# An octonion FFN kernel: the statistics of the third group of rows in the opening, a dot product and a ternary step moved on VectorE

## The chip, the cores and the metric

The kernel runs on one core of a Trainium2 chip. What is measured is the device time of the whole program in microseconds. TensorE (PE) does the matmuls, VectorE (DVE), ScalarE (ACT) and GpSimd (POOL) the elementwise work, SyncE (SP) issues the DMAs. Each engine runs its own list of instructions in order, and the lists meet at semaphores.

## The reference, cut to what matters

```python
x = L0_attn_x                                  # 1 x 2048 x 1024, f32
xn = layernorm(x, eps=1e-5)                    # per row, over 1024
attn = autocorrelation(xn)                     # rfft, irfft of |f|^2, top 6 lags, softmax, rolled rows
def ternary_dequant(W):
    scale = mean(abs(W))
    return scale * clip(round(W / scale), -1, 1)
def oct_ternary_linear(xp, W):                 # 8 octonion components, signs of S_OCT
    M = einsum('jik,jod->koid', S_OCT, ternary_dequant(W))
    return einsum('...id,koid->...ko', xp, M)
gate = oct_ternary_linear(xn, w_gate)          # 8 x 342 x 128
up   = oct_ternary_linear(xn, w_up)            # 8 x 342 x 128
h    = silu(gate) * up
out  = oct_ternary_linear(h, w_down)           # 8 x 128 x 342
return x + attn + out
```

The kernel computes for the attention part a bound that tells whether a row's lag 0 takes all of the softmax; then that part is xn itself, and out = x + xn + FFN. For rows where the bound fails there is a slow loop, which does not run for these inputs.

## The kernel before, in words

The 2048 rows of x are worked in 8 groups of 256 rows (G = 8), each in two tiles of 128 rows (NT = 2). The hidden size of 342 per component is cut in 3 chunks, c = 0 to 2. A group's work is cut into units, which TensorE takes in the order of the list `units`:

- ("T", m, c): transposes of a weight chunk (m = 0 gate, 1 up, 2 down), only in the opening. ScalarE then takes the signs (`signs`), DVE makes the ternary values (`ternary`) and sums and differences of them (`weight_slots`), and ScalarE multiplies two of the forms by 8 (`eights`) and makes negated copies (`negate`).
- ("X", g, half): transposes of the normalised x of group g; ScalarE and DVE split it into a high and a low f16 part, and its sums too (`x_high`, `x_low`, `x_adds`, `x_sums_high`, `x_sums_low`).
- ("G", g, c, Y) and ("U", g, c, Y): gate and up products of group g, chunk c. In group 0, chunks 0 and 1 are done directly (`direct`, line 407), all others by a cheaper scheme in two halves, "spectral" (line 380) and "terms" (line 387), between which ScalarE copies the odd parts to `pk` (`odd_two`) and DVE does four adds, then four more.
- ("F", g): the spectrum of group g and `lags`, whose minimum DVE takes with `least`.
- ("N", g, t): the down product of a tile (line 484).

The units share four pairs of PSUM banks; `take_banks` waits until the owner before has been read. For a ("T", ...) unit that is the end of its `ternary`, for ("F", g) the end of `least`, for a ("U", ...) unit the end of `product`.

The products h = silu(gate) * up are numbered in the order of the ("U", ...) units: number 0 is ("U", 0, 0, 0), 2 is ("U", 0, 1, 0), 6 is ("U", 1, 0, 0). DVE makes each (`product`, line 1100). GpSimd then does six operations on it, in the order of the numbers: four sums (1344, 1345, 1349, 1350) and two low parts (1352, 1355), with high parts by ScalarE (`h_high` line 743, `h_sums_high` line 754). ("N", 0, 0) needs the numbers 0 to 5.

The statistics of a group's rows are: `row_sum` on ScalarE for both tiles, and the negated mean (lines 603, 606); `row_var`, squares on ScalarE (617); `rstd`, eight small instructions on GpSimd (1301 to 1314); `normalise` on ScalarE (622), in place in `xr`; and `dot` on DVE (962), which is part of the bound. `xr` holds one group. `load_x(g)` on SP waits until the group before is transposed and its dots are done. The opening up to some 87 us is an order written out by hand for each engine; behind it one loop over the units runs on each engine, with tables (`sum_at`, `var_at`, `norm_at`, `dot_at`, `rstd_at`) that say at which unit a step of the statistics stands. Group 0 and 1 have their sums and squares in the opening, all others in the loop, one group ahead of use.

`junk` is a scratch of f16 for outputs nobody reads, but it holds also the negated weights of ("T", 1, 1) from about 59 us until the last direct product. `eights_no` numbers the eights in ScalarE's order; TensorE and SP wait for that count.

Of the kernel before, what the change touches and what calls it, by code (L numbers as in the profile page):

```python
def octonion_ffn_attention_kernel(nc, x, w_gate, w_up, w_down, dft, lag, out):
# [13 lines left out]
    T = 256  # L15
    NT = T // P
    G = ROWS // T
# [90 lines left out]
    slots_no = {("T", *t): i for i, t in enumerate(((0, 2), (1, 0), (1, 2), (0, 1), (1, 1), (2, 0), (2, 1), (2, 2)))}  # L108
    eights_no = {("T", *t): i for i, t in enumerate(((0, 2), (1, 2), (0, 0), (1, 0), (2, 0), (0, 1), (2, 1), (2, 2), (1, 1)))}
    g_no, u_no, n_no = rank("G"), rank("U"), rank("N")  # L110
# [19 lines left out]
    for g in range(2, G):  # L130
        a, b = g - 2, g - 1
        sum_at[place["G", b, 0, 0]] = g
        var_at[place["U", b, 0, 0]], var_at[place["G", b, 0, 1]] = (g, 0), (g, 1)
        rstd_at[u_no["U", b, 0, 0]] = g
        norm_at[place["N", b - 1, 0]] = g
        dot_at[place["N", b - 1, 1]] = g
# [27 lines left out]
    with ctx:  # L164
# [427 lines left out]
        def _(act):  # L592
# [3 lines left out]
            act.wait_ge(table_in, 1)  # L596

            def row_sum(g, t):
                k = NT * g + t
                act.wait_ge(x_in[t], 16 * (g + 1))  # L600
                act.wait_ge(sum_done, k - 1)
                act.wait_ge(var_done, NT * g)
                nc.scalar.activation(junk[:, :], xr[:, t, :], ACT.Copy, accum_out=sm[:, k:k + 1]).then_inc(sum_done, 1)
                if t == NT - 1:
                    act.wait_ge(sum_done, k)
                    nc.scalar.activation(nm[:, NT * g:NT * g + NT], sm[:, NT * g:NT * g + NT], ACT.Copy, scale=-1.0 / D).then_inc(mean_done, 1)

            def row_var(g, t):
                k = NT * g + t
                if g:  # L610
                    act.wait_ge(mean_done, g)
                    act.wait_ge(sum_done, NT * g + 1)
                else:
                    act.wait_ge((first_mean, second_mean)[t], 1)
                if k:
                    act.wait_ge(var_done, k)
                nc.scalar.activation(junk[:, :], xr[:, t, :], ACT.Square, bias=nm[:, k:k + 1], accum_out=vr[:, k:k + 1]).then_inc(var_done, 1)

# [66 lines left out]
            def odd_two(u):  # L685
# [4 lines left out]
                if q >= 2:  # L690
                    act.wait_ge(l1_done, 4 * q - 4)
                if u[0] == "X":
                    act.wait_ge(x_mm, x_no[u] + 1)
                    if u[1] == 0:

                        act.wait_ge(xlo_done, x_no[u] + 1)
                else:
                    act.wait_ge(spec_mm, sums_no[u] + 1)
# [110 lines left out]

            eights(("T", 0, 0))  # L810
            eights(("T", 1, 0))
            eights(("T", 2, 0))
            signs(("T", 2, 2))
            eights(("T", 0, 1))
            eights(("T", 2, 1))
            eights(("T", 2, 2))
            h_high(("U", 0, 1, 0))

            for n in range(OPEN, N + 8):
# [59 lines left out]
        def _(dve):  # L879
# [269 lines left out]
            product(("U", 0, 0, 0))  # L1149
            least(("F", 0))  # L1150
            ternary(("T", 0, 1))
            weight_slots(("T", 0, 1))
            ternary(("T", 1, 1))
            thresholds(2, ("T", 1, 1))
# [3 lines left out]
            ternary(("T", 2, 0))  # L1158
            x_sums_low(("X", 1, 0))
            x_low(("X", 1, 1))  # L1160
            x_adds(("X", 1, 1))
# [8 lines left out]
            product(("U", 0, 1, 0))  # L1170
            dot(1, 0)
            dot(1, 1)
            out_scales()
# [217 lines left out]
```

## Time and profile before

| | |
|---|---|
| median of 3 runs | 601.26 us (600.38 to 601.67) |
| profiled execution | 600.0 us, span 598.0 us |
| PE busy | 581.9 us, 97% of the span |
| DVE busy | 510.3 us, 85% |
| POOL busy | 457.8 us, 77% |
| ACT busy | 356.8 us, 60% |
| granted clock of TensorE | 1.000 |
| longest share of the chain that ended last | POOL 53%, issue 30%, PE 14% |

The span runs from the first to the last instruction; the rest of an execution's time lies around it. A busy share is a mean over stages. Where TensorE's idle time lies, and what released it, is read from the gaps in order of time.

### The profile page before, as it was taken

The numbers are of one execution on the slowest core, as the hardware profiler recorded it, in microseconds if no ns is written. First come the engines' busy times: TensorE is split into PE (matmuls) and PEld (weight loads), VectorE is DVE, ScalarE is ACT, GpSimd is POOL, SyncE is SP. The second block draws the span as 40 slices with busy tenths as digits, with TensorE's granted clock in tenths as the row PEclk, the third lists the DMA queues.
The fourth block names the chain that finished last, engine by engine and source line by source line (L and its number), as shares of the span: only waits on it lengthen the run. The fifth ranks groups of instructions, "written<-read, shape, count | busy, mean of one in ns | idle before, by whom it ended". The sixth has DMA issues, their size and how long they took to land.

```text
span 598.0 us, 16440 instructions
## 1 busy us (share of the span) xinstructions
PE 581.9 (97%) x6764; PEld 541.2 (91%) x6764; DVE 510.3 (85%) x1230; ACT 356.8 (60%) x497; POOL 457.8 (77%) x362
## 2 busy tenths in 40 slices
PE   7998999989999999999999999999999999999996
PEld 7998998878989999899989998899989998998996
DVE  4885898869998999979998999979998999967854
ACT  4677867674566546774566546764576555543540
POOL 3415739999779977999779977999679977997920
PEclk9999999999999999999999999999999999999999
DMA  9720012001220013002110014002220102002011
GB/s 213 157 72 1 1 46 98 2 1 72 72 71 2 37 38 136 7 2 71 73 72 1 37 37 142 1 2 73 71 72 2 63 12 71 2 3 71 1 72 73
DMA packets 10252, 30.67 MB, mean 51 GB/s; under 512 B 929, under 2 KB 4033, under 8 KB 10177
## 3 DMA queue, kind: packets, MB, share of 16 engines
q1 hardware_dynamic: 10176, 29.62, 15.4%
q8 instruction: 53, 0.87, 0.6%
q14 instruction: 23, 0.18, 0.1%
HBM read 21.23 MB, written 8.39 MB: 50 GB/s over the span
## 4 chain that ended last, share of the span: by engine, by line
POOL 53%; issue 30%; PE 14%; DVE 1%; POOLq 0%; ACT 0%; ACTq 0%
POOL hop L1355 16%; POOL hs L1349 10%; POOL hs L1345 10%; POOL hs L1350 9%; POOL hs L1344 6%; PE acc L484 5%; PE acc L407 4%; PE acc L416 2%; PE acc L387 1%; POOL r L1303 1%; POOL hop L1352 1%; PE acc L461 1%; PE acc L380 0%; POOL hop L1285 0%; PE acc L424 0%
## 5 line engine op out<-in xcount | busy, mean ns | idle before, releaser
L484 PE MATMUL acc<-wd,hop 114*128 114x128 f16 (+1 forms) x2944 | 170.7, 219 | 1.5 <-POOL hop L1355 1.2
L484 PEld LDWEIGHTS acc<-wd,hop 114*128 114x128 f16 (+1 forms) x2944 | 167.3, 98 | 2.9 <-POOL hop L1355 1.4
L699 ACT ACTIVATE pk<-acc 114x512 f32<-114x512 f32 (+1 forms) x120 | 70.9, 590 | 87.8 <-PE acc L380 53.2
L1344 POOL TENSOR_TENSOR hs<-hx 114x512 f32<-114x512 f32 x47 | 60.2, 1282 | 71.6 <-DVE hx L1100 64.0
L1355 POOL TENSOR_TENSOR hop<-hs,hop 114x1024 f16<-114x1024 f32 x46 | 98.2, 2135 | 2.3 <-ACT hop L754 2.3
L1352 POOL TENSOR_TENSOR hop<-hx,hop 114x1024 f16<-114x1024 f32 x46 | 98.3, 2138 | 0.6 <-ACT hop L743 0.6
L1003 DVE TENSOR_TENSOR bd<-acc,pk 114x256 f32<-114x256 f32 (+1 forms) x104 | 43.4, 417 | 51.3 <-ACT pk L699 51.3
L380 PE MATMUL acc<-xop,wu 128*128 128x256 f16 x704 | 84.2, 273 | 1.0 <-DVE hx L1100 0.7
L380 PE MATMUL acc<-xop,wg 128*128 128x256 f16 x704 | 84.1, 273 | 1.0 <-DVE hx L1100 0.9
L387 PE MATMUL acc<-xop,wu 128*128 128x256 f16 x704 | 84.1, 273 | 0.1
L387 PE MATMUL acc<-xop,wg 128*128 128x256 f16 x704 | 84.0, 273 | 0.1
L754 ACT ACTIVATE hop<-hs 114x1024 f16<-114x1024 f32 x46 | 48.5, 1055 | 55.0 <-POOL hs L1350 54.9
L380 PEld LDWEIGHTS acc<-xop,wu 128*128 128x128 f16 x704 | 67.8, 98 | 11.9 <-DVE dmin L1105 1.9
L380 PEld LDWEIGHTS acc<-xop,wg 128*128 128x128 f16 x704 | 67.7, 98 | 10.1 <-DVE hx L1100 2.4
L387 PEld LDWEIGHTS acc<-xop,wg 128*128 128x128 f16 x704 | 68.8, 98 | 8.3 <-issue 0.4
L387 PEld LDWEIGHTS acc<-xop,wu 128*128 128x128 f16 x704 | 67.6, 98 | 9.2 <-DVE acc L1051 1.8
L743 ACT ACTIVATE hop<-hx 114x1024 f16<-114x1024 f32 x46 | 48.4, 1051 | 29.2 <-DVE hx L1100 29.2
L1100 DVE SCALAR_TENSOR_TENSOR hx<-hx,few,acc 114x1024 f32<-114x1024 f32 x47 | 59.8, 1271 | 3.4 <-PE acc L407 1.8
L1349 POOL TENSOR_TENSOR hs<-hs 114x512 f32<-114x512 f32 x47 | 59.8, 1273 | 3.7
L1345 POOL TENSOR_TENSOR hs<-hx 114x512 f32<-114x512 f32 x47 | 60.4, 1284 | 0.0
L1350 POOL TENSOR_TENSOR hs<-hs 114x512 f32<-114x512 f32 x47 | 59.9, 1274 | 0.0
L1007 DVE TENSOR_TENSOR acc<-acc,pk 114x256 f32<-114x256 f32 (+1 forms) x104 | 43.8, 421 | 0.0
(164 smaller groups left out, 931.0 us busy)
## 6 DMA issues: line engine op xcount, KB each, us to landing
xr<-in_x SPq DMA_DIRECT2D x16, 512.0 KB, 4.4
zx<-in_x SPq DMA_DIRECT2D x16, 512.0 KB, 3.7
out_y<-zx SPq DMA_DIRECT2D x16, 512.0 KB, 2.6
hop<-in_w_down SPq DMA_DIRECT2D x1, 1364.0 KB, 18.9
hop<-in_w_gate SPq DMA_DIRECT2D x2, 576.0 KB, 9.3
hop<-in_w_up SPq DMA_DIRECT2D x1, 1152.0 KB
hop<-in_w_gate SPq DMA_DIRECT2D x1, 192.0 KB
hop<-in_w_up SPq DMA_DIRECT2D x1, 192.0 KB
```

The source lines that it names most:

```text
L380: last = nc.tensor.matmul(acc[:, bank[n], s // 2, T * (s % 2):T * (s % 2 + 1)], wm[:, c, slot, :], xop[:, g % 2, form, level, :], start=s ...
L387: last = nc.tensor.matmul(acc[:, bank[n], s // 2, T * (s % 2):T * (s % 2 + 1)], wm[:, c, slot, :], xop[:, g % 2, form, level, :], start=Fa ...
L484: last = nc.tensor.matmul(acc[:, bank[n], s // 2, at:at + P], operand(g, c, t, form, level), wd[0:WIDE[c], slot, c, :], start=which == 0 a ...
L699: nc.scalar.activation(pk[0:rows, q % 2, :, :], pair[:, :, T:2 * T], ACT.Copy, scale=XS if u[0] == "X" else 1.0).then_inc(copied, 1)
L754: nc.scalar.activation(half_of(g, c, NJ + 4 * Y, 0), by_tile(sums), ACT.Copy).then_inc(hhs_done if m < LAST else tail_high, 1)
L1100: nc.vector.scalar_tensor_tensor(hx[0:CH, m % 4, :, :], hx[0:CH, m % 4, :, :], scale[0:CH, :], bank_pair(place[u], CH).rearrange("p b (i t ...
L1344: nc.gpsimd.tensor_tensor(hs[:, 4:8:2, :], h[:, 0:4:2, :], h[:, 1:4:2, :], ALU.add)
L1345: nc.gpsimd.tensor_tensor(hs[:, 5:8:2, :], h[:, 0:4:2, :], h[:, 1:4:2, :], ALU.subtract).then_inc(hpair_done, 1)
L1349: nc.gpsimd.tensor_tensor(hs[:, 0:2, :], hs[:, 4:6, :], hs[:, 6:8, :], ALU.add).then_inc(hs_done, 1)
L1350: nc.gpsimd.tensor_tensor(hs[:, 2:4, :], hs[:, 4:6, :], hs[:, 6:8, :], ALU.subtract).then_inc(hs_done, 1)
L1352: nc.gpsimd.tensor_tensor(half_of(g, c, 4 * Y, 1), by_tile(h), half_of(g, c, 4 * Y, 0), ALU.subtract).then_inc(h_free, 1)
L1355: nc.gpsimd.tensor_tensor(half_of(g, c, NJ + 4 * Y, 1), by_tile(hs[:, 0:4, :]), half_of(g, c, NJ + 4 * Y, 0), ALU.subtract).then_inc(h_rea ...
```

## The change

- Group 2's `row_sum` and `row_var` are taken out of the loop's tables and written into ScalarE's opening, behind `silu(("G", 0, 1, 1))`. They write their scratch output to `pk` (f32), since `junk` is in use; `odd_two` of ("G", 0, 2, 0), the next writer of `pk`, waits for them.
- The eights of ("T", 0, 0), ("T", 1, 0) and ("T", 0, 1) move behind `h_high(("U", 0, 1, 0))`, with `eights_no` in the new order.
- `rstd(2)` on GpSimd moves from ahead of product 6 to ahead of product 2.
- On DVE the dots of group 1 move ahead of `x_low(("X", 1, 1))`, and with them the time at which SP can ask for group 2's x.
- On DVE `least(("F", 0))` moves behind the ternary and the slots of ("T", 0, 1).

```diff
@@ -106,7 +106,7 @@
     x_no, f_no, t_no = rank("X"), rank("F"), rank("T")
 
     slots_no = {("T", *t): i for i, t in enumerate(((0, 2), (1, 0), (1, 2), (0, 1), (1, 1), (2, 0), (2, 1), (2, 2)))}
-    eights_no = {("T", *t): i for i, t in enumerate(((0, 2), (1, 2), (0, 0), (1, 0), (2, 0), (0, 1), (2, 1), (2, 2), (1, 1)))}
+    eights_no = {("T", *t): i for i, t in enumerate(((0, 2), (1, 2), (2, 0), (2, 1), (2, 2), (0, 0), (1, 0), (0, 1), (1, 1)))}
     g_no, u_no, n_no = rank("G"), rank("U"), rank("N")
 
     LAST = len(u_no) - 1
@@ -129,9 +129,13 @@
     sum_at, var_at, rstd_at, norm_at, dot_at = {}, {}, {}, {}, {}
     for g in range(2, G):
         a, b = g - 2, g - 1
-        sum_at[place["G", b, 0, 0]] = g
-        var_at[place["U", b, 0, 0]], var_at[place["G", b, 0, 1]] = (g, 0), (g, 1)
-        rstd_at[u_no["U", b, 0, 0]] = g
+        if g == 2:
+
+            rstd_at[u_no["U", 0, 1, 0]] = g
+        else:
+            sum_at[place["G", b, 0, 0]] = g
+            var_at[place["U", b, 0, 0]], var_at[place["G", b, 0, 1]] = (g, 0), (g, 1)
+            rstd_at[u_no["U", b, 0, 0]] = g
         norm_at[place["N", b - 1, 0]] = g
         dot_at[place["N", b - 1, 1]] = g
     rstd_at[0] = 1
@@ -595,12 +599,18 @@
             nc.scalar.activation(junk[:, 0:1], ones[:, 0:1], ACT.Silu).then_inc(table_in, 1)
             act.wait_ge(table_in, 1)
 
+            def dump(g):
+                return pk[:, :, :, :].rearrange("p a i t -> p (a i t)") if g == 2 else junk[:, :]
+
             def row_sum(g, t):
                 k = NT * g + t
                 act.wait_ge(x_in[t], 16 * (g + 1))
                 act.wait_ge(sum_done, k - 1)
                 act.wait_ge(var_done, NT * g)
-                nc.scalar.activation(junk[:, :], xr[:, t, :], ACT.Copy, accum_out=sm[:, k:k + 1]).then_inc(sum_done, 1)
+                if g == 2:
+
+                    act.wait_ge(l1_done, 16)
+                nc.scalar.activation(dump(g), xr[:, t, :], ACT.Copy, accum_out=sm[:, k:k + 1]).then_inc(sum_done, 1)
                 if t == NT - 1:
                     act.wait_ge(sum_done, k)
                     nc.scalar.activation(nm[:, NT * g:NT * g + NT], sm[:, NT * g:NT * g + NT], ACT.Copy, scale=-1.0 / D).then_inc(mean_done, 1)
@@ -614,7 +624,7 @@
                     act.wait_ge((first_mean, second_mean)[t], 1)
                 if k:
                     act.wait_ge(var_done, k)
-                nc.scalar.activation(junk[:, :], xr[:, t, :], ACT.Square, bias=nm[:, k:k + 1], accum_out=vr[:, k:k + 1]).then_inc(var_done, 1)
+                nc.scalar.activation(dump(g), xr[:, t, :], ACT.Square, bias=nm[:, k:k + 1], accum_out=vr[:, k:k + 1]).then_inc(var_done, 1)
 
             def normalise(g, t):
                 k = NT * g + t
@@ -689,6 +699,8 @@
                 pair = bank_pair(place[u], rows)
                 if q >= 2:
                     act.wait_ge(l1_done, 4 * q - 4)
+                if u == ("G", 0, 2, 0):
+                    act.wait_ge(var_done, 3 * NT)
                 if u[0] == "X":
                     act.wait_ge(x_mm, x_no[u] + 1)
                     if u[1] == 0:
@@ -807,14 +819,18 @@
             eights(("T", 1, 2))
             silu(("G", 0, 1, 1))
 
-            eights(("T", 0, 0))
-            eights(("T", 1, 0))
+            row_sum(2, 0)
+            row_sum(2, 1)
             eights(("T", 2, 0))
             signs(("T", 2, 2))
-            eights(("T", 0, 1))
+            row_var(2, 0)
+            row_var(2, 1)
             eights(("T", 2, 1))
             eights(("T", 2, 2))
             h_high(("U", 0, 1, 0))
+            eights(("T", 0, 0))
+            eights(("T", 1, 0))
+            eights(("T", 0, 1))
 
             for n in range(OPEN, N + 8):
                 if n in norm_at:
@@ -1147,9 +1163,9 @@
             weight_slots(("T", 1, 2))
 
             product(("U", 0, 0, 0))
-            least(("F", 0))
             ternary(("T", 0, 1))
             weight_slots(("T", 0, 1))
+            least(("F", 0))
             ternary(("T", 1, 1))
             thresholds(2, ("T", 1, 1))
             product(("U", 0, 0, 1))
@@ -1157,6 +1173,8 @@
             x_adds(("X", 1, 0))
             ternary(("T", 2, 0))
             x_sums_low(("X", 1, 0))
+            dot(1, 0)
+            dot(1, 1)
             x_low(("X", 1, 1))
             x_adds(("X", 1, 1))
             ternary(("T", 2, 1))
@@ -1168,8 +1186,6 @@
             ternary(("T", 2, 2))
             weight_slots(("T", 2, 2))
             product(("U", 0, 1, 0))
-            dot(1, 0)
-            dot(1, 1)
             out_scales()
             product(("U", 0, 1, 1))
```

DVE, behind product 0, at some 44 us: before, `least` (L1105) stands ahead of the ternary of ("T", 0, 1) (L929).

```order
L954 TENSOR_TENSOR wu<-zx 128x4x113 x3
L1100 SCALAR_TENSOR_TENSOR hx<-hx,few,acc 114x1024 [waits silu_done,term_mm]
L1105 TENSOR_REDUCE dmin<-acc 128x2 [waits lag_mm]
L929 SCALAR_TENSOR_TENSOR wg<-acc,few,zx 128x4x114 [waits sign_done] x2
L946 TENSOR_TENSOR zx<-wg 128x2x2x114 [waits tern_done]
L947 TENSOR_TENSOR zx<-wg 128x2x2x114
L954 TENSOR_TENSOR wg<-zx 128x4x114 [waits pairs_done]
L954 TENSOR_TENSOR wg<-zx 128x4x114 x3
L929 SCALAR_TENSOR_TENSOR wu<-acc,few,zx 128x4x114 [waits sign_done] x2
L895 TENSOR_REDUCE few<-acc 128x1 [waits total_mm]
```

The same piece of DVE's list in the changed kernel, whose line numbers are up to 16 higher:

```order
L970 TENSOR_TENSOR wu<-zx 128x4x113 x3
L1116 SCALAR_TENSOR_TENSOR hx<-hx,few,acc 114x1024 [waits silu_done,term_mm]
L945 SCALAR_TENSOR_TENSOR wg<-acc,few,zx 128x4x114 [waits sign_done] x2
L962 TENSOR_TENSOR zx<-wg 128x2x2x114 [waits tern_done]
L963 TENSOR_TENSOR zx<-wg 128x2x2x114
L970 TENSOR_TENSOR wg<-zx 128x4x114 [waits pairs_done]
L970 TENSOR_TENSOR wg<-zx 128x4x114 x3
L1121 TENSOR_REDUCE dmin<-acc 128x2 [waits lag_mm]
L945 SCALAR_TENSOR_TENSOR wu<-acc,few,zx 128x4x114 [waits sign_done] x2
L911 TENSOR_REDUCE few<-acc 128x1 [waits total_mm]
```

`least` (now L1121) stands behind the two ternaries and the six operations of the slots.

ScalarE, behind `silu(("G", 0, 1, 1))`, at some 74 us: before, eights (L682, into wg, wu and wd) and the signs of ("T", 2, 2) (L654).

```order
L682 ACTIVATE wg<-wg 128x114 [waits neg_done,term_mm,first_pairs,tern_done]
L682 ACTIVATE wg<-wg 128x3x114
L682 ACTIVATE wg<-wg 128x2x114 x2
L682 ACTIVATE wu<-wu 128x114 [waits neg_done,term_mm,pairs_done,tern_done]
L682 ACTIVATE wu<-wu 128x3x114
L682 ACTIVATE wu<-wu 128x2x114 x2
L682 ACTIVATE wd<-zx 114x4x128 [waits tern_done]
L682 ACTIVATE wd<-zx 114x2x128 x3
L654 ACTIVATE zx<-acc,few 113x512 [waits pairs_done,tern_done,eights_done,thr_done2,wt_mm]
L654 ACTIVATE zx<-acc,few 113x512
L682 ACTIVATE wg<-wg 128x114 [waits neg_done,term_mm,pairs_done,tern_done]
L682 ACTIVATE wg<-wg 128x3x114
```

The same twelve places in the changed kernel:

```order
L613 ACTIVATE pk,sm<-xr 128x1024 [waits var_done,l1_done,sum_done,x_in0]
L613 ACTIVATE pk,sm<-xr 128x1024 [waits var_done,l1_done,sum_done,x_in1]
L616 ACTIVATE nm<-sm 128x2 [waits sum_done]
L692 ACTIVATE wd<-zx 114x4x128 [waits tern_done]
L692 ACTIVATE wd<-zx 114x2x128 x3
L664 ACTIVATE zx<-acc,few 113x512 [waits pairs_done,tern_done,eights_done,thr_done2,wt_mm]
L664 ACTIVATE zx<-acc,few 113x512
L627 ACTIVATE pk,vr<-xr,nm 128x1024 [waits var_done,sum_done,mean_done] x2
L692 ACTIVATE wd<-zx 114x4x128 [waits tern_done]
L692 ACTIVATE wd<-zx 114x2x128 x3
L692 ACTIVATE wd<-zx 113x4x128 [waits tern_done]
L692 ACTIVATE wd<-zx 113x2x128 x3
```

The sums (L613) and squares (L627) of group 2 stand among the eights of the down weights (L692, into wd); the eights into wg and wu follow behind the high part, which is the next row.

GpSimd, ahead of product 2, at some 84 us: before, its first sum (L1344) follows the low part of product 1 (L1355).

```order
L1350 TENSOR_TENSOR hs<-hs 114x512
L1352 TENSOR_TENSOR hop<-hx,hop 114x2x4x128 [waits hhi_done]
L1355 TENSOR_TENSOR hop<-hs,hop 114x2x4x128 [waits hs_done,hhs_done]
L1344 TENSOR_TENSOR hs<-hx 114x2x256 [waits hs_done,h_done]
L1345 TENSOR_TENSOR hs<-hx 114x2x256
```

And in the changed kernel:

```order
L1366 TENSOR_TENSOR hs<-hs 114x512
L1368 TENSOR_TENSOR hop<-hx,hop 114x2x4x128 [waits hhi_done]
L1371 TENSOR_TENSOR hop<-hs,hop 114x2x4x128 [waits hs_done,hhs_done]
L1317 TENSOR_SCALAR vr<-vr 128x2 [waits ln_done,var_done]
L1319 TENSOR_TENSOR r<-vr,mh 128x2 [waits newton]
L1321 TENSOR_TENSOR rr<-r 128x2 [waits newton]
L1323 TENSOR_TENSOR rr<-rr,vr 128x2 [waits newton]
L1325 TENSOR_SCALAR rr<-rr 128x2 [waits newton]
L1327 TENSOR_TENSOR rs<-r,rr 128x2 [waits newton]
L1329 TENSOR_TENSOR nmrs<-nm,rs 128x2 [waits newton]
L1330 TENSOR_SCALAR onep<-rs 128x2
L1360 TENSOR_TENSOR hs<-hx 114x2x256 [waits hs_done,h_done]
```

The eight instructions of `rstd(2)` (L1317 to L1330), the first with a wait for all squares of group 2, now stand ahead of it.

## Rows read from the trace of the kernel before

**Rows 1.** busy time by stretch (start:end us, length, busy us of each engine, granted clock, DMA)

```profile
87.00:110.00 23.00, 22.74 (x207) 19.79 (x205) 19.78 (x51) 16.56 (x27) 22.77 (x16) 1.00 0.25 93
...
145.00:440.00 295.00, 294.67 (x3523) 271.23 (x3521) 272.98 (x660) 179.67 (x239) 249.02 (x191) 1.00 0.15 53
```

**Rows 2.** TensorE in order of time: start us, us, engine line operation [idle before <-releaser]

```profile
50.36 1.00 PE L461 MATMUL acc<-ident,hop 114*128 114x114 f32 x8 [1.99 <-DVE wg L929]
...
122.07 1.96 PE L484 MATMUL acc<-wd,hop 113*128 113x128 f16 x32 [1.21 <-POOL hop L1355]
...
130.22 1.09 PE L424 MATMUL acc<-ident,xr 128*128 128x128 f32 x8 [0.95 <-DVE hx L1100]
...
131.56 5.54 PE L484 MATMUL acc<-wd,hop 114*128 114x128 f16 x96 [0.24 <-DVE acc L1025]
...
143.20 1.92 PE L380 MATMUL acc<-xop,wg 128*128 128x256 f16 x16 [0.86 <-DVE hx L1100]
```

**Rows 3.** in order of time, ScalarE, TensorE and DVE from 44 to 50 us

```profile
44.49 1.18 ACT L654 ACTIVATE zx<-acc,few 128x456 f16<-128x456 f32 x2 [0.19 <-PE acc L461]
...
47.78 0.60 PE L445 MATMUL acc<-lag_sb,pw 128*128 128x256 f16 x4
...
48.01 2.36 ACT L622 ACTIVATE xr<-xr,nmrs,rs 128x1024 f32<-128x1024 f32 x2
...
48.42 0.69 DVE L1105 TENSOR_REDUCE dmin<-acc 128x2 f32<-128x512 f32 x1 [3.87 <-PE acc L445]
...
49.03 1.28 DVE L929 SCALAR_TENSOR_TENSOR wg<-acc,few,zx 128x456 f16<-128x456 f32 x2
```

**Rows 4.** in order of time, DVE from 62 to 84 us

```profile
62.66 1.21 DVE L1092 TENSOR_TENSOR xop<-acc,xop 128x1024 f16<-128x1024 f32 x1
...
66.51 1.22 DVE L1083 SCALAR_TENSOR_TENSOR xop<-acc,xop 128x1024 f16<-128x1024 f32 x1 [2.64 <-ACT xop L703]
...
82.88 1.27 DVE L1100 SCALAR_TENSOR_TENSOR hx<-hx,few,acc 114x1024 f32<-114x1024 f32 x1
```

**Rows 5.** in order of time, ScalarE and GpSimd: group 1's pass, then 72 to 79 us

```profile
37.56 1.06 ACT L603 ACTIVATE junk<-xr 128x1024 f16<-128x1024 f32 x1
...
42.89 0.19 POOL L1301 TENSOR_SCALAR vr<-vr 128x2 f32<-128x2 f32 x1 [17.26 <-ACT junk L617]
...
72.80 1.10 ACT L728 ACTIVATE hx<-acc,few 114x1024 f32<-114x1024 f32 x1
...
76.06 1.54 ACT L682 ACTIVATE wd<-zx 114x512 f16<-114x512 f16 x4
...
77.72 1.27 ACT L654 ACTIVATE zx<-acc,few 113x512 f16<-113x512 f32 x2
```

**Rows 6.** in order of time, GpSimd from 84 to 134 us

```profile
84.23 1.65 POOL L1344 TENSOR_TENSOR hs<-hx 114x512 f32<-114x512 f32 x1 [12.51 <-DVE hx L1100]
...
122.10 0.19 POOL L1301 TENSOR_SCALAR vr<-vr 128x2 f32<-128x2 f32 x1
...
124.60 1.27 POOL L1344 TENSOR_TENSOR hs<-hx 114x512 f32<-114x512 f32 x1
...
133.84 1.28 POOL L1344 TENSOR_TENSOR hs<-hx 114x512 f32<-114x512 f32 x1
```

**Rows 7.** in order of time, ScalarE at 124 and 138 us

```profile
124.68 2.37 ACT L622 ACTIVATE xr<-xr,nmrs,rs 128x1024 f32<-128x1024 f32 x2 [3.32 <-POOL onep L1314]
...
138.96 1.06 ACT L754 ACTIVATE hop<-hs 114x1024 f16<-114x1024 f32 x1 [4.20 <-POOL hs L1350]
```

**Rows 8.** the dots: line 962 (ns min/median/max), then one in order of time

```profile
L962 DVE SCALAR_TENSOR_TENSOR dj<-xr x16: 681/693/2227, 30.4 to 486.3; 128x512 f16<-128x512 f32 x16
...
84.88 1.56 DVE L962 SCALAR_TENSOR_TENSOR dj<-xr 128x512 f16<-128x512 f32 x1
```

**Rows 9.** tile xr from 0 to 160 us, time of its loads to landing

```profile
DMA to landing us min/median/max: 3.4/4.1/5.7
```

**Rows 10.** DMA issues of the page: operation, KB each, us to landing

```profile
hop<-in_w_down SPq DMA_DIRECT2D x1, 1364.0 KB, 18.9
```

## The prediction, made before the changed kernel ran

> **What bounds the kernel now.** I read the busy time by stretch first, then the gaps of TensorE in order of time, then the chain of waits that ended last, and from each gap back along the engine it waits for. From 145 to 440 us TensorE is busy 294.67 of 295.00 us at a granted clock of 1.00 [rows 1]: in the steady state there is nothing to win but matmuls, and the change takes none away. What is left are five gaps of TensorE between 50 and 144 us [rows 2]: 1.99 us ahead of the transposes of the fifth weight unit ("T", 1, 1), then 1.21, 0.95, 0.24 and 0.86 us around the first down product ("N", 0, 0). Behind each gap TensorE stays busy up to the tail of the run, so a microsecond taken out of a gap should reach the end whole, provided that the next engine in line is early enough.
>
> The gap at 50.36 is released by DVE's ternary of ("T", 0, 1) [rows 2]. DVE had been idle 3.87 us before the minimum over the lags, which waits for TensorE's lag matmuls, and only behind it does it do the ternary, though ScalarE's signs for it ran from 44.49 to 45.67 [rows 3].
>
> The other four gaps hang on GpSimd. From 87 to 110 us it is busy 22.77 of 23.00 us [rows 1]: its h work begins at 84.23 and runs without a pause. Four products (numbers 2 to 5) end at about 122.0, and the 1.21 us gap at 122.07 is TensorE waiting for the last of them [rows 2, 6]. Then GpSimd does the eight small instructions of group 2's reciprocal root, 122.10 to 124.60 [rows 6]. ScalarE stands in front of the normalisation for 3.32 us until they are done [rows 7], everything behind it in its queue (the copy of ("N", 0, 0)'s odd parts) is late, DVE's adds and product are late by it, and TensorE gets the 0.95 and the 0.24. Product 7's sums, another 2.5 us late for the same reason, hold ScalarE for 4.20 us at 138.96 [rows 7] and give the 0.86.
>
> **The change part by part.**
> *Ternary ahead of the minimum.* DVE is free at 48.42 - 3.87 = 44.55, the signs are there by 45.67, two ternaries take 1.28 us [rows 3]: done at about 46.5 instead of 50.3. TensorE ends the lag matmuls at 47.78 + 0.60 = 48.38 [rows 3] and goes on at once: the whole 1.99 us, less a semaphore's 0.04, that is 1.95. What is late next: ScalarE is normalising group 1 until 48.01 + 2.36 = 50.37 [rows 3] before it can do the signs of ("T", 1, 1), so those come 1.3 instead of 1.95 us earlier; TensorE needs that bank only for ("T", 2, 0), behind a half of a direct product, ("X", 1, 0) and another half. The minimum, now behind the slots, still ends before 50; its bank is wanted only by ("G", 0, 1, 0). No instruction is added.
>
> *Dots of group 1 moved up.* They now stand between DVE's low sums of ("X", 1, 0), ending at 62.66 + 1.21 = 63.87, and the low part of ("X", 1, 1) at 66.51, before which DVE is idle for 2.64 us [rows 4]; shifted by 1.95 that is a hole from 61.9 to 64.56. A dot alone takes 0.69 us, beside GpSimd up to 2.23 (a median of 693 ns over 16) [rows 8], so the pair costs 1.5 to about 4.6 us (twice 0.69 or twice 2.23, and the reads of the accumulators). The trace shows the second dot beside GpSimd's sums at 1.56, and GpSimd's first sum at 84.23 then takes 1.65 instead of 1.27 [rows 6, 8]. One such dot of 1.56 beside one of 0.69 makes about 2.4 us, one of 2.23 beside one of 0.69 some 3.1, and I take this stretch, the nearer rows' 2.4 and at most 3.1: nothing to 0.5 us late at 64.56, which passes straight through DVE's unbroken work to the product at 82.88. At the far end it is 2.0 us late.
>
> The Trainium skill ("SBUF — State Buffer", SBUF: two separate sides) says that a VectorE operation with two SBUF inputs and a GpSimd operation exclude each other for a whole instruction, so that the loser waits and does not merely slow down. The trace agrees: 1.65 against 1.27 us. By that rule each moved dot waits for the GpSimd sum that is then running, the pair ends about 65.1, and the sum below is worth 0.1 to 0.2 us less; it also says that GpSimd's products at 84 us are freed of the dots.
>
> *Group 2's x earlier.* The load waits for the dots and for the transposes of ("X", 1, 1); with the dots done at 64.3 to 65.0 its two DMAs go out on SP's queue there instead of at 86.5, and land after 3.4 to 5.7 us [rows 9], by 71 at the latest. Nothing else is on the queue then; the two loads of zx behind it move up as well, their readers stand behind ("N", 0, 0).
>
> *Sums and squares in the opening.* ScalarE comes to the first sum where it began the eights of ("T", 0, 0), one microsecond behind the silu at 72.80 [rows 5], that is 73.80 - 1.95 = 71.85: x has landed. For group 1 it took from 37.56 to 42.89, 5.33 us, from the first sum to the start of the root [rows 5]. Now 1.54 us of down eights and 1.27 us of signs (pipelined, 2.7 together [rows 5]) lie within, so that the root begins at about 79.9 and ends 2.5 us later, at 82.4. The scratch is now f32 and not f16; no row shows that copy. The nearest with an f32 output is the normalisation, 2.36 / 2 = 1.18 us [rows 3], while the four passes of group 1 come to 5.33 / 4 = 1.33 each with all that goes with them, so I take no difference; the ends are zero and, were each pass 0.1 longer, 0.4 us in all. The signs of ("T", 2, 2) come about 0.4 us later than a plain shift; DVE asks for them later still. High part of product 2: up to 1.2 us later, but GpSimd wants it only behind four sums of 1.27 us.
>
> *The eights of three units behind the high part.* Three times about 1.2 us. They fill the idle time in which ScalarE waited for the first half of ("G", 0, 2, 0) and may run a few tenths past it, which makes DVE and TensorE as much late; TensorE meets GpSimd at ("N", 0, 0) anyway and has more than that to wait there, so it costs nothing; without that wait it would cost those tenths. Nobody reads these eights before group 1.
>
> *GpSimd.* Product 2 is ready for it at 82.88 + 1.27 - 1.95 = 82.2 [rows 4], or 82.8 with late dots; the root ends at 82.4. I take a start at 82.6 against 84.23: 1.6 us. Without the dots beside it the four products take 4 x 9.24 = 37.0 us (124.60 to 133.84 for one [rows 6]) and not 122.0 - 84.23 = 37.8: 0.8 more. So GpSimd is 2.4 us earlier at ("N", 0, 0): TensorE, 1.95 early, waits 0.76 there and not 1.21, and is 2.4 ahead. Behind it the root is gone from GpSimd's queue, which leaves it 4.9 ahead and ScalarE free of the 3.32 us: the normalisation runs at about 119, ("N", 0, 0)'s odd parts are copied as soon as TensorE ends, product 7 is done by 125, TensorE wants its bank at 130.22 - 0.95 - 2.4 = 126.9. Gaps of 0.95 and 0.24 go. At the last, product 8 follows from GpSimd's product 7 sums 4.9 us earlier, at 143.2 - 4.9 = 138.3, and TensorE arrives at 142.34 - 2.4 - 1.19 = 138.75: the 0.86 goes too, with 0.4 to spare.
>
> Sum: 2.4 + 0.95 + 0.24 + 0.86 = 4.45, say 4.4 us. The profiled execution took 600.0 us (span 598.0 and 2.0 around it), so it would take 595.6; it lay 1.26 under the median of 601.26, which gives **596.9 us**. With all five gaps gone (5.2) it is 596.1.
>
> **The rivals.**
> *A, the shared port or a late chain on DVE.* Both dots blocked in full (4.6 us), or the signs of ("T", 2, 2) late: product 2 ends at 84.2, GpSimd gains only the 0.8, the later gaps still go: 0.8 + 2.05 = 2.9 us, 598.4. For it: the 2.23 of rows 8. Against: only one dot of each pair is that slow, since GpSimd's sums there last 1.27 and not 2.1.
> *B, only the opening gap.* The stretch behind ("N", 0, 0) is held by something that four gaps now hide, DVE above all, and TensorE only keeps what ("T", 1, 1) gave: 2.0 us, 599.3. For it: those gaps end with DVE. Against: each time DVE had itself been waiting for ScalarE, and ScalarE for GpSimd [rows 7].
> *C, slower.* The root of group 2 now stands in front of product 2 on GpSimd, which has no slack up to 144 us, and ScalarE's queue stops at the sum if x is late. Every microsecond that x comes after 71.85 costs one: 4.4 late gives back all, 5.6 makes it slower by the bound. With the 18.9 us of the down weights [rows 10] it would land at 84, 12 late: 4.4 - 12 = -7.6, 608.9. Against: those 18.9 were in a full queue; the x loads take at most 5.7.
> *D, nothing changes.* The gaps turn up again elsewhere: 601.3.
>
> **How the numbers follow.** Forecast 0.65, A 0.13, B 0.10, C 0.06, D 0.06. About 0.2%, 1.2 us, is what can be told from no change. Faster: the forecast, A and most of B, 0.87; within: D and a little of B, 0.07; slower: 0.06. The range runs from all five gaps with half a microsecond of scatter, 595.6, to just behind B, 599.5; C and D are left out.
>
> **What would show it.** No gap of TensorE at the transposes of ("T", 1, 1); the load of x at about 65; the dots inside DVE's hole before the low part of ("X", 1, 1), with the product behind at 81 to 81.6; the root on GpSimd from 80 to 82.5, with the first sum of product 2 right behind it at 1.27 us; one gap of 0.5 to 0.9 at ("N", 0, 0), released by GpSimd, and none behind it up to the tail. Wrong would be a gap with ScalarE or a DMA as its releaser, a root that ends after 84, or gaps between 150 and 510 us.

## The result, and the profile after

| | before | after |
|---|---|---|
| median | 601.26 us (5 runs, 600.38 to 601.76) | 595.38 us (5 runs, 594.52 to 595.56) |
| profiled execution, span | 600.0 us, 598.0 us | 595.38 us, 593.3 us |
| mean granted clock of TensorE | 1.000 | 0.999 |

The changed kernel is faster: ratio 0.9901, 95% interval 0.989 to 0.9912, 5.9 us. The prediction said 596.9 us, 595.6 to 599.5, so the time lies 0.2 us below its range. The sign and the mechanism are as forecast, the size is not. All ratios leave out one execution, of `e1_gap_filled`, that took 1016 us at a mean granted clock of 0.558.

TensorE of the changed kernel in order of time, every row from 20 to 150 us that has a gap ahead of it (start us, us, engine, line, operation, in brackets the idle time and its releaser):

```profile
91.41 1.91 PE L391 MATMUL acc<-xop,wg 128*128 128x256 f16 x16 [0.15 <-DVE acc L1059]
...
119.92 1.96 PE L488 MATMUL acc<-wd,hop 113*128 113x128 f16 x32 [0.74 <-POOL hop L1371]
```

Of the five gaps of [rows 2] one is left, at the first down product, and it is 0.74 us (forecast: 0.76). The gap ahead of the transposes of ("T", 1, 1) is gone, and so are the three behind the down product. The 0.15 us at 91.41 is no new delay: the kernel before has the same wait (its matmul rows of 91.05 and 93.09 start 2.04 us apart, these 2.07), and the moved eights are not its cause, since ScalarE had waited 0.53 us for TensorE before the copy at 87.88 that DVE's adds need.

Around the first gap, DVE and TensorE of the changed kernel:

```profile
45.66 1.29 DVE L945 SCALAR_TENSOR_TENSOR wg<-acc,few,zx 128x456 f16<-128x456 f32 x2 [0.61 <-ACT zx L664]
...
48.28 0.60 PE L449 MATMUL acc<-lag_sb,pw 128*128 128x256 f16 x4
...
48.71 0.95 PE L465 MATMUL acc<-ident,hop 114*128 114x114 f32 x8
...
48.96 0.68 DVE L1121 TENSOR_REDUCE dmin<-acc 128x2 f32<-128x512 f32 x1
```

The ternary (L945) starts at 45.66 and no longer waits for the lag matmuls (L449, 48.28); the transposes (L465) follow these at once, at 48.71 against 50.36 in [rows 2]. The minimum (L1121) comes at 48.96, as forecast before 50.

DVE, SP, ScalarE and GpSimd of the changed kernel, the dots, the load of x, its first sum, the root and product 2:

```profile
62.09 1.25 DVE L978 SCALAR_TENSOR_TENSOR dj<-xr 128x512 f16<-128x512 f32 x1
...
63.46 1.55 DVE L978 SCALAR_TENSOR_TENSOR dj<-xr 128x512 f16<-128x512 f32 x1
...
65.10 0.80 SPq L318 DMA_DIRECT2D xr<-in_x  x2
...
72.23 1.05 ACT L613 ACTIVATE pk<-xr 128x1024 f32<-128x1024 f32 x1
...
80.22 0.22 POOL L1317 TENSOR_SCALAR vr<-vr 128x2 f32<-128x2 f32 x1 [10.19 <-ACT pk L627]
...
82.91 1.27 POOL L1360 TENSOR_TENSOR hs<-hx 114x512 f32<-114x512 f32 x1
...
119.81 1.30 POOL L1360 TENSOR_TENSOR hs<-hx 114x512 f32<-114x512 f32 x1
```

Each stands within half a microsecond of where the prediction put it (load at about 65, first sum 71.85, root 79.9 to 82.4, product 2 at 82.6), though the whole trace lies 0.5 us late from the start (below). The dots took 1.25 and 1.55 us, beside GpSimd, and product 2 begins with a sum of 1.27 us where [rows 6] had 1.65. GpSimd's four products end at 119.8 against 122.0.

The gaps are 5.25 us of idle time before and 0.89 after, 4.36 less. Yet the two traces part by more. These are the same TensorE instructions in the two traces, by the start of the row:

| first row of | before | after | before - after |
|---|---|---|---|
| the transposes of ("T", 0, 0), behind the 76 idle ones | 13.88 | 14.38 | -0.50 |
| the transposes of ("T", 1, 1) | 50.36 | 48.71 | 1.65, and 1.70 behind them |
| the last third of ("N", 0, 0) | 122.07 | 119.92 | 2.15 |
| the transposes of ("X", 2, 0) | 130.22 | 126.96 | 3.26 |
| the terms of ("N", 0, 0) | 131.56 | 127.84 | 3.72 |
| ("G", 1, 2, 0) | 143.20 | 138.50 | 4.70 |

From there on the difference stays at 4.68 us until the last output. It is the 0.5 us lost at the start and 5.2 us won behind it. A gap thus costs more than its idle time: 2.20 for 1.99, 1.11 for 0.95, 0.46 for 0.24, 0.98 for 0.86. In a stretch without gaps a row of 1.91 us is followed by the next one 1.75 us after its start, since the end of a matmul is modelled as lying behind the start of the next; the matmuls behind a gap do not overlap those ahead of it. The difference from start to start counts that, the idle time does not.

That leaves two questions: why the medians part by 5.9 us and the profiled executions by 4.6, and what the 0.5 at the start is.

### The profile page after: what moved, and what is told of

Read it like the earlier page. It is cut to its first block, busy times and chain, and to the rows that moved or that the text cites. A ratio compares the mean times of both kernels' runs of the same rounds, so it can differ in the third digit from the quotient of the medians.

```text
span 593.3 us, 16442 instructions
## 1 busy us (share of the span) xinstructions
PE 581.7 (98%) x6764; PEld 541.9 (91%) x6764; DVE 510.1 (86%) x1230; ACT 357.0 (60%) x497; POOL 457.5 (77%) x362
## 4 chain that ended last, share of the span: by engine, by line
POOL 50%; issue 28%; PE 7%; ACT 1%; DVE 1%; POOLq 0%; ACTq 0%
POOL hop L1371 15%; POOL hs L1365 9%; POOL hs L1361 9%; POOL hs L1366 9%; PE acc L488 5%; POOL hs L1360 5%; PE acc L391 1%; POOL r L1319 1%; ACT pk L627 0%; ACT pk L613 0%; POOL hop L1368 0%; PE acc L384 0%; ACT wd L692 0%; POOL onep L1330 0%; POOL vr L1317 0%
```

## The experiments

Each ran beside the kernel before on the same chip. Line numbers of a fence are those of its own kernel.

### The two kernels once more

`a0_before_again` and `a1_after_again` are the two kernels, unchanged.

> The kernel before once more, word for word, for a second trace of it. In the first pair of traces TensorE's 76 idle transposes at the start took 10.52 us before and 11.02 after, and all that follows carries this 0.5 us. Theory 1 (the start varies from run to run, whatever the kernel; the change is worth what the trace shows behind it, 5.2 us): a second trace of the same kernel can start with either value, and its span is 598.0 or about 598.5. Theory 2 (the 11.02 belongs to the changed kernel, since its program is another): 10.52 again, span 598.0. In both the ratio to before is 1.000.

> The changed kernel once more. Theory 1: the stretch at the start may be 10.5 or 11.0; where it is 10.5 the span is about 592.8, and 5.2 us of 601.3 make a ratio of 0.9913. Theory 2: 11.02 again and span 593.3. Theory 3 (the medians differ by more than the traces because the first profile of before was a lucky one): the ratio is again 0.990 with a before of 601.3, and other profiles of before lie near 599.3 in span.

Measured: 601.10 us, ratio 0.9999 (0.9991 to 1.0008), and 595.12 us, ratio 0.9902 (0.9887 to 0.9916). The 76 idle transposes of TensorE at the start took 10.52 us in the first trace of the kernel before, 10.98 in the second and 10.40 in a third; in the changed kernel 11.02 and 10.69:

```profile
3.52 10.98 PE L416 MATMUL acc<-ident 128*128 128x128 f32 x76 [3.52 <-POOL ident L1290]
```

```profile
3.53 10.69 PE L420 MATMUL acc<-ident 128*128 128x128 f32 x76 [3.53 <-POOL ident L1306]
```

So the 0.5 us at the start belong to the execution and not to the kernel: theory 1. The rows of the shortest and the longest of these starts (10.10 us in b1, 11.21 us in c1) show where they part (first the stretch, its length and the busy time of PE with its count):

```profile
6.00:8.00 2.00, 2.00 (x16) 2.00 (x15) 0.94 (x1) 1.20 (x2) 0.00 (x0) 1.00 1.09 147
...
6.00:8.00 2.00, 2.00 (x11) 2.00 (x10) 1.37 (x2) 1.04 (x3) 0.00 (x0) 1.00 1.07 176
```

From 6 to 8 us TensorE did 16 of the idle transposes in b1 and 11 in c1. In each of the 14 traces it does 4 or 5 in half a microsecond at first and 7 later, and the pace changes at a time between 7 and 9 us that differs by execution. The granted clock reads 1.00 in both rows, so what changes the pace the profile does not name.

Theory 3, that the first profile of before was a lucky one, is right in part: the second one has a span of 598.4 us, not 599.3. What the times of single executions showed is more: the 12 of a0 fall in two clusters, six with a span of 597.9 to 598.8 us at a mean granted clock of 0.997 to 0.998 and six with 599.1 to 599.7 at 0.995 to 0.996. The nine executions of the changed kernel lie between 592.5 and 593.5 at 0.999 to 1.000.

### One half of the change, and the other

```diff
 # b1_ternary_only: the kernel before, with
-            least(("F", 0))
             ternary(("T", 0, 1))
             weight_slots(("T", 0, 1))
+            least(("F", 0))
 # b2_all_but_ternary: the changed kernel, with the opposite edit
```

> The kernel before with nothing but the ternary and slots of (T, 0, 1) ahead of the minimum. Theory 1: the 1.99 us gap at 50 us goes; counted from start to start of the matmuls on either side it cost 2.2 us, and GpSimd's start at product 2, which follows DVE, moves with it, so that the four later gaps stay as they are: 2.2 us faster, ratio 0.9963. Rival (GpSimd is the bound at the first down product, whatever TensorE does): the gap at 122 us grows by what was won, nothing at the end, ratio 1.000. Rival (a gap costs its idle time only): 1.99 us.

> The changed kernel with the minimum over the lags back ahead of the ternary of (T, 0, 1). Theory 1: the gap at 50 us is back at 2.0 us of idle time and 2.2 in cost; the root ends at about 84.8, GpSimd starts product 2 there, some 0.5 later than before, but saves the 0.8 of the dots: 0.8 to 0.9 us of gap at the first down product, the 0.95, 0.24 and 0.86 gone. 3.0 us faster than before, ratio 0.995. Rival (the two parts need each other, since the root alone now holds GpSimd): less than 1.5 us faster.

Measured: b1 597.70 us, ratio 0.9949 (0.9936 to 0.9962), 3.1 us faster, where 2.2 were expected; b2 597.68, ratio 0.9946 (0.9934 to 0.9958), 3.2 us, where 3.0 were expected. TensorE in b1:

```profile
119.69 1.96 PE L484 MATMUL acc<-wd,hop 113*128 113x128 f16 x32 [1.20 <-POOL hop L1355]
...
127.85 1.09 PE L424 MATMUL acc<-ident,xr 128*128 128x128 f32 x8 [0.95 <-DVE hx L1100]
...
129.19 5.54 PE L484 MATMUL acc<-wd,hop 114*128 114x128 f16 x96 [0.25 <-DVE acc L1025]
...
140.80 1.92 PE L380 MATMUL acc<-xop,wg 128*128 128x256 f16 x16 [0.83 <-DVE hx L1100]
```

All four later gaps are as in [rows 2]: GpSimd moved along with DVE, and the rival that it would stand still fell. In the trace b1 is 2.2 us ahead of before behind the transposes of ("T", 1, 1), the start taken out, and keeps it; that is theory 1's sum. But the median gained 0.9 more than the trace. In b2 the gap at 50 us stayed (1.99 us), the later ones became one of 0.61 us, and the trace gained 3.1, as the median did. So the extra microsecond seems to come with the gap at 50 us. And b2 has executions at 0.995 and 0.996 again (two of six), b1 none of five.

### The gap at 50 us, filled and looked at

```diff
 # e1_gap_filled: the kernel before, with
             lags(("F", 0))
+            pe.wait_ge(h_done, 1)
+            idle_work(14)
             weights(("T", 1, 1))
```

The wait for `h_done` holds the idle transposes until DVE has made product 0, so that they fall into the gap.

> The kernel before with 14 idle transposes on TensorE ahead of the transposes of (T, 1, 1), in the gap at 50 us; nothing else moves. Of the runs so far, the executions of the kernel before differ: span about 598.2 at a granted clock of 0.998, about 599.5 at 0.995 to 0.996; the kernel with all but the ternary step shows both as well, while the changed kernel and the one with the ternary alone, both without the gap at 50, stay at 0.999 and over in all 14 executions. Theory 1 (in some executions the idle time at 50 us makes the granted clock fall, which costs 1.2 us): with the gap filled the trace is as before, but no execution lies under 0.997, and the median falls by 0.6 to 1.2 us: ratio 0.998 to 0.999. Theory 2 (the spread comes from elsewhere, the start or the tail): both kinds of executions as before, ratio 1.000.

Measured: 600.17 us against 600.81, ratio 0.9989 (0.998 to 0.9998). Of its ten executions beside the one of 1016 us none lies under a clock of 0.997, while of the 23 of the kernel before beside it ten lie at 0.995 to 0.996, with spans of 599.1 to 599.7. The trace behind the gap is the old one:

```profile
50.38 1.00 PE L461 MATMUL acc<-ident,hop 114*128 114x114 f32 x8 [0.46 <-DVE wg L931]
...
122.06 1.96 PE L484 MATMUL acc<-wd,hop 113*128 113x128 f16 x32 [1.18 <-POOL hop L1357]
```

The transposes start at 50.38 as before and the down product waits as before, 122.06. So 0.6 us of the median (0.1 to 1.2 by the interval) went by giving TensorE something to do in 1.5 us in which it had only waited. To see where it had gone, `f1_before_look` and `f2_before_look` are two more profiled executions of the kernel before, and `f3_all_but_ternary_look` one of b2.

> The kernel before, one look. If the look catches an execution at a granted clock of 0.995 or 0.996, theory 1 has the granted clock under 1.00 for some microseconds behind the 1.99 us gap at 50 us, the matmuls there at up to twice their time, and all that follows 1.1 to 1.3 us later. Theory 2 has the low clock at the start or in the tail, theory 3 behind the gaps at 122 to 143 us. At 0.998 and over it tells nothing new.

> The kernel before, a second look, for the same question: an execution at 0.995 or 0.996 shows where the clock is low. Theory 1: behind the 1.99 us gap at 50 us. Theory 2: at the start or in the tail. Theory 3: behind the gaps at 122 to 143 us.

> The kernel with all but the ternary step, one look; two of its six executions lay at 0.995 to 0.996. As f1: theory 1 has the low clock behind the gap at 50 us, 1.99 us long, where this kernel is like the one before; theory 3 leaves it no place, since of the gaps at 122 to 143 us only one of 0.61 us is left.

f2 (600.35 us) and f3 (597.52) had 0.998 and told nothing new. f1 was an execution at 0.996, 601.53 us. Its busy time from 48 to 58 us (start:end us, length, busy us of PE, PEld, DVE, ACT, POOL with counts, then the granted clock, DMA share, GB/s):

```profile
48.00:50.00 2.00, 0.27 (x3) 0.00 (x0) 1.70 (x3) 2.00 (x3) 0.00 (x0) 1.00 0.00 0
50.00:52.00 2.00, 1.75 (x16) 1.75 (x17) 1.93 (x7) 0.70 (x2) 0.00 (x0) 0.95 0.00 0
52.00:54.00 2.00, 2.00 (x12) 2.00 (x11) 1.75 (x5) 2.00 (x4) 1.56 (x2) 0.50 0.00 0
54.00:56.00 2.00, 2.00 (x15) 2.00 (x14) 0.00 (x0) 0.52 (x1) 1.92 (x2) 0.69 0.00 0
56.00:58.00 2.00, 2.00 (x21) 2.00 (x20) 1.28 (x1) 0.44 (x1) 2.00 (x3) 1.00 0.00 0
```

and its TensorE in order of time:

```profile
50.25 1.00 PE L461 MATMUL acc<-ident,hop 114*128 114x114 f32 x8 [1.98 <-DVE wg L929]
...
51.24 3.96 PE L407 MATMUL acc<-xop,wu 128*114 128x256 f16 x20
55.00 1.59 PE L407 MATMUL acc<-xop,wd 128*114 128x256 f16 x12
```

TensorE was idle for 1.98 us ahead of 50.25, and 1.5 us later the granted clock is at 0.50, the lower of its two levels, 1.2 GHz; it is back at 1.00 by 56. The 20 matmuls at 51.24 took 3.96 us; in the first trace, at a clock of 1.00, the same 20 took 2.37 from 51.35. At the next transposes this execution is 1.66 us behind the first one, the start taken out, and it stays there. Elsewhere up to the tail its clock is 1.00, behind the gaps at 122 to 143 us too. So theory 1 is shown: f1 has the fall behind this gap in plain sight, and with the gap filled (e1) no execution has the low mean clock.

Whether the clock falls there differs from execution to execution. Of the 69 executions of the kernel before whose mean clock is on record here, 34 have 0.995 or 0.996, with a median of 601.52 us, and 35 have 0.997 or more, with a median of 600.51. The nine of the changed kernel have 595.21: 5.3 us less than the quicker kind, close to the 5.2 of the traces, and 6.3 less than the other. The two kinds lie 1.0 us apart and not 1.66. One reason may be the start: that of f1 was short, 10.40 us against 10.98 in the second trace, and the two spans differ by 1.1. Whether a short start and the fall go together, one trace cannot show.

### The root's place on GpSimd

```diff
 # c1_root_late: the changed kernel, with
-            rstd_at[u_no["U", 0, 1, 0]] = g
+            rstd_at[u_no["U", b, 0, 0]] = g
```

> The changed kernel with group 2's root on GpSimd back ahead of product 6, its sums and squares still in the opening. Theory 1 (the place of the root in GpSimd's list makes the later gaps): product 2 starts when DVE has made it, 0.3 us earlier, so that the gap at the first down product is 0.4 instead of 0.74; then the 0.95, 0.24 and 0.86 are back, 2.5 us in cost, and the kernel is 2.2 us slower than the changed one: 597.3, ratio 0.994. Rival (those gaps went because ScalarE's sums and squares left the loop): as fast as the changed kernel, 0.990.

Measured: 597.71 us, ratio 0.9941 (0.9928 to 0.9954), 2.3 us slower than the changed kernel beside 2.2 expected.

```profile
119.83 1.96 PE L488 MATMUL acc<-wd,hop 113*128 113x128 f16 x32 [0.45 <-POOL hop L1371]
...
127.97 1.09 PE L428 MATMUL acc<-ident,xr 128*128 128x128 f32 x8 [0.94 <-DVE hx L1116]
...
129.31 5.54 PE L488 MATMUL acc<-wd,hop 114*128 114x128 f16 x96 [0.25 <-DVE acc L1041]
...
140.94 1.92 PE L384 MATMUL acc<-xop,wg 128*128 128x256 f16 x16 [0.85 <-DVE hx L1116]
```

The 0.45, 0.94, 0.25 and 0.85 were forecast as 0.4, 0.95, 0.24 and 0.86. ScalarE's sums and squares are in the opening here as well, so it is the root in GpSimd's list that makes the three later gaps, as the prediction had it, and the rival fell.

### x later

```diff
 # c2_x_late: the changed kernel, with
             x_sums_low(("X", 1, 0))
-            dot(1, 0)
-            dot(1, 1)
             ...
             x_sums_low(("X", 1, 1))
+            dot(1, 0)
+            dot(1, 1)
```

> The changed kernel with the dots of group 1 behind the low sums of (X, 1, 1) and not ahead of its low part, so that x is asked for at about 74 instead of 65 and lands at 78 to 79, where ScalarE has stood in front of the first sum since 72.2. Theory 1 (every microsecond that x is late passes through ScalarE, the root and GpSimd to the end): 6.3 us late, all of it at the first down product, part of it shown as a wait of (U, 0, 2, 0) for product 2: 601.4, ratio 1.001. Rival (GpSimd's idle time of 10 us ahead of the root and TensorE's direct products cover most of it): less than 3 us slower than the changed kernel, 0.995 or less.

Measured: 599.44 us, ratio 0.9977 (0.9968 to 0.9985), 4.3 to 4.5 us slower than the changed kernel, between theory and rival.

```profile
75.58 1.06 ACT L613 ACTIVATE pk<-xr 128x1024 f32<-128x1024 f32 x1 [4.28 <-DMA xr<-in_x]
...
86.33 1.27 POOL L1360 TENSOR_TENSOR hs<-hx 114x512 f32<-114x512 f32 x1
```

```profile
94.13 1.91 PE L391 MATMUL acc<-xop,wg 128*128 128x256 f16 x16 [3.77 <-DVE acc L1059]
...
123.30 1.96 PE L488 MATMUL acc<-wd,hop 113*128 113x128 f16 x32 [1.32 <-POOL hop L1371]
```

The price per microsecond was right, the lateness (6.3 us expected) was not. x came at 75.58, where ScalarE had stood for 4.28 us, since the dots, with no GpSimd beside them, took 0.68 and 0.69 us and the load went out at 72. That is 4.25 us later than in the changed kernel, the start taken out, and the trace is 4.28 us behind: every microsecond that x is late passed to the end. It passed earlier than expected, with 3.77 us of it as a wait for DVE's adds behind ScalarE's late copy, and of the eleven executions five have a mean clock of 0.992 and two of 0.995. No trace shows where in these it was low; the median holds that loss too, so the price is read from the trace alone.

### The dots alone

```diff
 # b3_dots_only: the kernel before, with
             x_sums_low(("X", 1, 0))
+            dot(1, 0)
+            dot(1, 1)
             x_low(("X", 1, 1))
             ...
             product(("U", 0, 1, 0))
-            dot(1, 0)
-            dot(1, 1)
```

> The kernel before with nothing but the dots of group 1 ahead of the low part of (X, 1, 1). Theory 1 (the dots beside GpSimd's first sums of product 2 cost GpSimd 0.8 us, and GpSimd is what the gap at the first down product waits for): product 2's two first sums take 1.27 us each instead of 1.65 and 1.71, the gap at 122 us falls from 1.21 to 0.4, the other four stay: 0.8 us faster, ratio 0.9987, too near to the scatter for the times alone, but plain in the trace. Rival (the two dots hold up DVE in their new place and product 2 comes later by as much): the gap at 122 us stays at 1.0 to 1.2, no faster.

Measured: 600.83 us, ratio 0.9993 (0.9984 to 1.0002), not told from no change. In the trace:

```profile
84.80 1.27 POOL L1344 TENSOR_TENSOR hs<-hx 114x512 f32<-114x512 f32 x1 [12.42 <-DVE hx L1100]
86.03 1.27 POOL L1345 TENSOR_TENSOR hs<-hx 114x512 f32<-114x512 f32 x1
...
110.73 2.14 POOL L1355 TENSOR_TENSOR hop<-hs,hop 114x1024 f16<-114x1024 f32 x1 [0.30 <-ACT hop L754]
```

```profile
122.15 1.96 PE L484 MATMUL acc<-wd,hop 113*128 113x128 f16 x32 [0.72 <-POOL hop L1355]
```

GpSimd's first sums take 1.27 each, it is 0.8 us ahead at the next product, and the gap fell from 1.21 to 0.72. 0.30 us were given back at 110.73, where GpSimd waited for ScalarE (L754), which in this kernel has group 2's squares among the loop's copies. So the dots are worth 0.5 us alone and 0.8 where the sums and squares have left the loop too: from the first sum of product 2 to the end of product 5 GpSimd took 37.8 us before, 37.3 here and 36.9 in the changed kernel. Of the eleven executions six have a clock of 0.996, as the gap at 50 us is still there.

### A version meant to beat both

```diff
 # d1_product_first: the changed kernel, with
-            ternary(("T", 2, 2))
-            weight_slots(("T", 2, 2))
             product(("U", 0, 1, 0))
+            ternary(("T", 2, 2))
+            weight_slots(("T", 2, 2))
 # and on ScalarE
+            row_var(2, 0)
+            row_var(2, 1)
             eights(("T", 2, 0))
             signs(("T", 2, 2))
-            row_var(2, 0)
-            row_var(2, 1)
```

> The changed kernel with two more moves: DVE makes product 2 ahead of the ternary and slots of (T, 2, 2), and ScalarE does the squares of group 2 ahead of the eights of (T, 2, 0) and the signs of (T, 2, 2). Theory 1 (what is left of the gap at the first down product, 0.74 us, is GpSimd's start at product 2, which its root and DVE's product set at 82.9 and 82.6): the root ends at 80.1, product 2 at 80.4, GpSimd starts 2.5 us earlier and the gap goes: 0.74, with the refilling of TensorE's pipeline up to 0.9 us faster than the changed kernel: 594.3, ratio 0.9885. Rival (the late high parts or the late ternary of (T, 2, 2) take it back): the same as the changed kernel or slower, 0.990.

Measured: 597.59 us, ratio 0.9938 (0.9926 to 0.995), 2.2 us slower than the changed kernel.

```profile
80.13 1.27 POOL L1360 TENSOR_TENSOR hs<-hx 114x512 f32<-114x512 f32 x1 [0.21 <-DVE hx L1116]
```

```profile
81.40 1.51 DVE L962 TENSOR_TENSOR zx<-zx 113x512 f16<-113x512 f16 x1
82.83 1.49 DVE L963 TENSOR_TENSOR zx<-zx 113x512 f16<-113x512 f16 x1
84.36 4.32 DVE L970 TENSOR_TENSOR wd<-zx 113x512 f16<-113x512 f16 x4
```

```profile
93.30 3.49 PE L391 MATMUL acc<-xop,wg 128*128 128x256 f16 x16 [2.35 <-ACT wu L692]
```

GpSimd did start product 2 at 80.13, 2.5 us earlier with the start taken out, and the gap at the down product went. But the sums of the slots, which before ran while GpSimd was idle, now ran beside it: 1.51, 1.49 and 4.32 us for what took 0.42, 0.42 and 1.43 in the kernel before. DVE was late for ("G", 0, 2, 0), and TensorE waited 2.35 us at 93.30. (The row names ScalarE's eights, which ended at 93.20; DVE's adds ended at 93.15, and in the changed kernel too TensorE starts 0.15 us behind them.) In this execution the clock fell to 0.50 behind that gap, and the 16 matmuls took 3.49 us instead of 1.91. Five of the six executions have a mean clock of 0.997 and took 597.5 to 598.0 us; the sixth has 1.000 and took 595.87, 0.7 us more than the changed kernel. So most of the 2.2 us goes with the clock. That two VectorE inputs in SBUF and a GpSimd operation keep each other out for a whole instruction is what the Trainium skill says ("SBUF — State Buffer", SBUF: two separate sides); the numbers here agree with it on VectorE's side, where operations of 0.42 us took up to 1.51; GpSimd's own lost less than 0.2 us each (its second two sums took 1.34 and 1.45 us instead of 1.27). Neither this nor another kernel tried beats the changed one.

## Why the prediction was wrong, by its own steps

- The five gaps, what releases each, and which of them go: right, gap by gap (0.74 left for 0.76 forecast), and b1, b2 and c1 showed each cause alone.
- The dots in DVE's hole, x at 65, sums, root and product 2: right to half a microsecond. The pair of dots took 2.9 us (62.09 to 65.03) and not 2.4, since both and not one of them ran beside GpSimd (1.25 and 1.55 us), but within the 3.1 allowed; DVE went on 0.15 us later than in c2, where no dot stands there. So rival A's price did not come up. Rival B fell with c1, since the later gaps go with the root. Rival C had the right price: c2 was 4.28 us slower for 4.25 us of x. The few tenths that the late eights might cost did not show either.
- "2.4 + 0.95 + 0.24 + 0.86 = 4.45": this step failed, by 0.75 us. The terms were mis-sized, since a gap was priced at its idle time. Counted from start to start of the same matmuls the 2.4 was 2.65 (2.20 for the first gap, where the sum had 1.95 with an unsourced 0.04 taken off that no row shows; 0.47 at the down product; less 0.02 at 91 us), and the others 1.11, 0.46 and 0.98: 5.2 us.
- "it lay 1.26 under the median of 601.26, which gives 596.9": this step failed too, by about as much. It carried the distance between one execution and the median over to a kernel in which a part of its cause is gone. That execution was one in which the clock had not fallen behind the gap at 50 us; in about half of all it falls. The changed kernel's profiled execution lies on its median, 595.38, and with the start of the first trace it would lie 0.5 under it, not 1.26. Filling the gap, with all else as it was, took 0.6 us off the median (e1). 5.2 and 0.6 make 5.8 of the 5.9 us measured; the last tenth is within the scatter.
- Each of the two alone would have left the forecast near 596.1, and the measured time 0.7 us off; together they make the 1.5 us between 596.9 and 595.4.
- The range ended at all five gaps by their idle time and half a microsecond, with nothing below for either of the two.

What stays open: how often the clock falls behind a gap of 2 us was counted by the mean clock of these executions only (34 of 69 for the kernel before, 6 of 11 for b3, 2 of 6 for b2), and what makes one of them fall and the next not, no trace shows. That the 0.9 us which b1 gained beyond its trace are this and nothing else follows from e1 and f1, but its interval is 0.8 us to either side. The fall itself was seen in one trace of the kernel before.

## What to carry to other kernels

Price a gap of TensorE from the start of the matmul ahead to the start of the one behind it, against the same pair without the gap. Before carrying the distance between a profiled execution and the median over to a changed kernel, look at the span and mean granted clock of every execution: two clusters were here the mark of something in the kernel that costs only sometimes, and the trace of a quick one did not show it. Where one engine runs without pause into the bound, look for short work in its list that could stand in an earlier pause of it, and look what runs beside it in the new place.

## What the runs showed that had not been expected

- A single gap of 1.98 us on TensorE, in a stretch otherwise full, was followed in f1 by about 3.5 us at a granted clock of 0.50, and about half of the kernel's executions have the mean clock that goes with it; with 0.46 us in its place (e1) none of ten has. A gap of 2.35 us in d1 was followed by the same.
- The same 76 idle transposes at the start of the program took from 10.10 to 11.21 us in 14 traces of kernels with the same opening, as their pace rose earlier or later, which moves everything behind them; two traces are compared from behind them.
